# A causal stage's masks move into the copies of turned weights, one product moves to VectorE, and the order is planned from other durations

## The reference

```python
dot = einsum('bhid,bhjd->bhij', q, k)                       # 16 heads of 16
vals = q_norm_sq + k_norm_sq.transpose(0, 1, 3, 2)
scores = dot * dot / (vals - 2.0 * dot + EPSILON)
scores = scores + triu(ones, k=1) * -1000000000.0           # causal
attn = softmax(scores, axis=-1)
out = einsum('bhij,bhjd->bhid', attn, v)
```

## Time and profile before

| | us |
|---|---|
| median of 3 runs | 5082.77 (5076.04 to 5086.52) |
| the profiled execution | 5068.32 |
| its span, first to last instruction | 5066.3 |
| PE, DVE, ACT, POOL busy | 4401.1, 3392.7, 2583.0, 2323.3 |
| TensorE clock, mean over the span | 0.924 of full |

### The profile page before, as it was taken

How to read it: one execution, slowest core, us unless ns; L and a number is a source line. 1 busy time by engine, 2 the same in 40 slices (tenths; PEclk the granted TensorE clock), 3 DMA queues, 4 the chain that set the end, 5 groups by cost and what they waited for, 6 DMA issues and landing times.

```text
span 5066.3 us, 65767 instructions
## 1 busy us (share of the span) xinstructions
PE 4401.1 (87%) x23008; PEld 2677.9 (53%) x23008; DVE 3392.7 (67%) x7648; ACT 2583.0 (51%) x5513; POOL 2323.3 (46%) x2203
## 2 busy tenths in 40 slices
PE   7888888999999999987787777777799999999997
PEld 3444445555555555554554454444555555555564
DVE  4454466666666666647889988999766666656553
ACT  4344344444444444427887777777444444444442
POOL 1111145455454454534555555565545444455441
PEclk9999999999999999997777777887899999999998
DMA  2000000000001000000000000100000000000000
GB/s 65 9 5 5 9 22 11 3 3 5 20 3 31 7 9 11 16 16 17 20 20 17 16 22 18 32 11 15 29 3 3 5 20 9 25 15 17 11 15 21
DMA packets 61208, 77.56 MB, mean 15 GB/s; under 512 B 13896, under 2 KB 45264, under 8 KB 60880
## 3 DMA queue, kind: packets, MB, share of 16 engines
q1 hardware_dynamic: 60880, 73.36, 5.0%
HBM read 35.61 MB, written 12.58 MB: 10 GB/s over the span
## 4 chain that ended last, share of the span: by engine, by line
PE 61%; DVE 21%; issue 7%; ACT 6%; POOL 4%; DMA 1%; SPq 1%; DVEq 0%; POOLq 0%; ACTq 0%
PE wide L725 44%; PE o_ps L725 8%; PE turn_ps L728 5%; PE wide L728 3%; DVE prob L1262 3%; DVE x L1256 2%; DVE pt L1299 2%; DVE prob L1273 2%; DVE hid L1256 1%; DVE x L1143 1%; DMA shifted<-resid 1%; DVE st L1280 1%; ACT pt L1106 1%; POOL rn L1443 1%; DVE w_up L1239 1%
## 5 line engine op out<-in xcount | busy, mean ns | idle before, releaser
L1477 POOL TENSOR_SCALAR prob<-prob,st 128x256 f32<-128x256 f32 (+1 forms) x1024 | 524.8, 533 | 976.9 <-DVE st L1286 976.6
L725 PE MATMUL wide<-x,w_up 128*128 128x512 f32 (+5 forms) x2560 | 943.5, 593 | 21.6 <-DVE k_t L1203 11.4
L725 PE MATMUL wide<-w_in,x_t 128*128 128x512 f32 (+1 forms) x1792 | 828.9, 607 | 6.5 <-DVE w_up L1246 3.1
L725 PE MATMUL o_ps<-pt,v 128*64 128x256 f32 (+2 forms) x5632 | 619.7, 369 | 118.6 <-DVE pt L1299 77.0
L1106 ACT ACTIVATE pt<-turn_ps 128x512 f32<-128x512 f32 x384 | 229.2, 597 | 854.1 <-PE turn_ps L728 854.1
L725 PEld LDWEIGHTS o_ps<-pt,v 128*64 128x64 f32 (+1 forms) x5632 | 394.6, 140 | 380.1 <-issue 191.2
L1075 ACT ACTIVATE prob<-prob,st 128x256 f32<-128x256 f32 (+1 forms) x1024 | 479.0, 472 | 194.7 <-DVE st L1273 194.5
L728 PE MATMUL turn_ps<-ident,prob 128*128 128x128 f32 x2816 | 465.3, 285 | 125.6 <-ACT pt L1106 121.9
L725 PEld LDWEIGHTS wide<-x,w_up 128*128 128x128 f32 (+2 forms) x2560 | 365.1, 200 | 375.5 <-issue 354.4
L728 PEld LDWEIGHTS turn_ps<-ident,prob 128*128 128x128 f32 x2816 | 315.1, 142 | 420.1 <-issue 238.0
L725 PEld LDWEIGHTS wide<-w_in,x_t 128*128 128x128 f32 x1792 | 339.9, 200 | 370.4 <-issue 363.8
(11 more groups left out here) (132 smaller groups left out, 7823.2 us busy)
## 6 DMA issues: line engine op xcount, KB each, us to landing
kept<-resid SPq DMA_DIRECT2D x16, 512.0 KB, 2.6
x<-kept SPq DMA_DIRECT2D x16, 512.0 KB, 3.3
...
```

Source lines behind the costliest of these rows:

```text
L725: return eng.matmul(out, lhsT, rhs, start=start, stop=stop, skip_group_check=True)
L1477: last = eng.tensor_scalar(pr[:, local_span(t)], pr[:, local_span(t)], sm[:, 8 + t:9 + t], 1.0, ALU.mult, ALU.mult)
```

## The change

It does four things. (1) `bclose` moves from POOL's queue to DVE's, one `tensor_tensor` over 768, 768 or 1024 columns. (2) `mask` is gone. The blocks on the diagonal are instead transposed into the half that DVE copies, and DVE's `pt_b` multiplies them by `causal_keep` (the transposed mask) as it reads them from PSUM; where that half holds other blocks too (i % 3 = 2), a second instruction copies these. (3) `B_TURNS` shares the blocks of both heads anew between the copies: ACT's takes 2, 4, 4 blocks for the three sorts of step (before 3, 3, 4), DVE's 4, 2, 4, of which 4, 2, 2 are masked. `turned_to` tells `mix` where a block lies. (4) All durations in `cost` are replaced, for stages a and f too, and the order of all queues is planned anew.

```diff
+B_TURNS = [([(0, 0), (1, 0)], [(0, 1), (0, 2), (1, 1), (1, 2)]),
+           ([(0, 0), (0, 1), (1, 0), (1, 1)], [(0, 2), (1, 2)]),
+           ([(0, 0), (0, 1), (1, 0), (1, 1)], [(0, 3), (1, 3), (0, 2), (1, 2)])]
+B_OWN = [4, 2, 2]
+def turned_to(i, k, block):
+    for half in range(2):
+        if (k, block) in B_TURNS[i % 3][half]:
+            return 512 * half + P * B_TURNS[i % 3][half].index((k, block))
...
-        return 2.8 if i % 2 else 0.0
+        return {"score": {"a": 1.92, "f": 1.72}, "mix": {"a": 2.4, "f": 1.68}}[kind][st] if i % 2 else 0.0
...
-            put("mask", k, at + 1 / steps, final("exp", k))
             for side in "ab":
-                put("turn_" + side, k, at + 2 / steps, final("mask", k))
+                put("turn_" + side, k, at + 2 / steps, final("exp", k))
...
                 elif kind in ("turn_a", "turn_b") and stage_of(u) == "b":
-                    pe.wait_ge(S["mask"], nth("mask", u, i))
-                    at, to = (0, 0) if kind == "turn_a" else (b_width(i), 512)
-                    for kb in range(b_width(i) // P):
-                        last = tr(ps[:, to + kb * P:to + (kb + 1) * P],
-                                  prob[SLOTS[u, i]["prob"]][:, at + kb * P:at + (kb + 1) * P])
+                    pe.wait_ge(S["exp"], nth("exp", u, i))
+                    for k, block in B_TURNS[i % 3][kind == "turn_b"]:
+                        to, at = turned_to(i, k, block), k * b_width(i) + block * P
+                        last = tr(ps[:, to:to + P], prob[SLOTS[u, i]["prob"]][:, at:at + P])
...
+                elif kind == "bclose":
+                    den, inv = [a[(o - 1) % 3][:, 0:2 * b_width(i)] for a in (b_den, b_inv)]
+                    dve.wait_ge(S["bguess"], o)
+                    eng.tensor_tensor(den, den, inv, ALU.mult).then_inc(S["bclose"], 1)
...
-                    w = {"f": 384, "a": 512, "b": b_width(i)}[stage_of(u)]
-                    ps = wide[PLACE["turn_b", u, i]][:, 512:1024] if stage_of(u) == "b" else turn_ps
-                    eng.tensor_copy(pt[:, 512:512 + w], ps[:, 0:w]).then_inc(S["pt_b"], 1)
+                    if stage_of(u) == "b":
+                        ps, met, n = wide[PLACE["turn_b", u, i]], P * B_OWN[i % 3], P * len(B_TURNS[i % 3][1])
+                        last = eng.tensor_tensor(blocks(pt[:, 512:512 + met]), blocks(ps[:, 512:512 + met]),
+                                                 causal_keep[:, :].unsqueeze(1).to_broadcast([P, met // P, P]), ALU.mult)
+                        if n > met:
+                            last = eng.tensor_copy(pt[:, 512 + met:512 + n], ps[:, 512 + met:512 + n])
+                        last.then_inc(S["pt_b"], 1)
...
-                elif kind == "bclose":
-                    pool.wait_ge(S["bguess"], o)
-                    eng.tensor_tensor(den, den, inv, ALU.mult).then_inc(S["bclose"], 1)
-                elif kind == "mask":
-                    pool.wait_ge(S["exp"], nth("exp", u, i))
-                    eng.tensor_tensor(at, at, ones, ALU.mult).then_inc(S["mask"], 1)
```

More of the change, by code:

```diff
@@ L89 @@
         "ACT": "xt_c raw v_c q_c aq_c lat_c av_c bsq bk_c bq_c bnum bguess exp pt_a out olog gelu",
-        "DVE": "bn_h nrm_h cos ss join k_c ak_c row bss bclip bmul low inv pt_b out_b res bn_f bn_f2 nrm_f xt2_c gate hid res2",
-        "POOL": "rstd_h sin rn brow bias_b bclose mask wt rstd_f bias back rot pad_out pad_down pad_v",
+        "DVE": "bn_h nrm_h cos ss join k_c ak_c row bss bclip bclose bmul low inv pt_b out_b res bn_f bn_f2 nrm_f xt2_c gate hid res2",
+        "POOL": "rstd_h sin rn brow bias_b wt rstd_f bias back rot pad_out pad_down pad_v",
         "SP": "load_in load_out load_rot load_up kept moved back_in store dup_a dup_b"}.items():
@@ L94 @@
         ENGINE[_k] = _e
-B_COST = {"bclip": (0.15, 0.27), "bnum": (0.1, 0.22), "bguess": (0.2, 0.47), "bclose": (0.2, 0.6), "bmul": (0.8, 0.6),
-          "exp": (0.85, 0.21), "turn_a": (0.03, 0.175), "turn_b": (0.03, 0.175), "pt_a": (0.06, 0.12),
-          "pt_b": (0.12, 0.135), "mix": (0.05, 0.34), "mask": (0.95, 0.0)}
+B_COST = {"bclip": (0.3, 0.27), "bnum": (0.1, 0.23), "bguess": (0.2, 0.48), "bclose": (0.1, 0.27), "bmul": (0.5, 0.53),
+          "exp": (0.85, 0.24), "mix": (0.05, 0.33)}
 def cost(kind, u, i):
@@ L105, in cost @@
     if kind in ("score", "mix") and st != "b":
-        return 2.8 if i % 2 else 0.0
+        return {"score": {"a": 1.92, "f": 1.72}, "mix": {"a": 2.4, "f": 1.68}}[kind][st] if i % 2 else 0.0
+    if kind in ("turn_a", "turn_b", "pt_a", "pt_b") and st == "b":
+        n = len(B_TURNS[i % 3][kind[-1] == "b"])
+        return {"turn": 0.03 + 0.17 * n, "pt_a": 0.1 + 0.12 * n, "pt_b": (0.26 if i % 3 == 2 else 0.13) + 0.135 * n}[
+            "turn" if kind[0] == "t" else kind]
     if kind in B_COST and st == "b":
@@ L109, in cost @@
     if kind in ("bden", "bdot"):
[L110 removed]
+        return 0.05 + 0.34 * b_width(i) / P if kind == "bdot" else 0.0
     by_stage = {
[L112 to L114 removed]
[3 rows of a table added]
     if kind in by_stage:
         return by_stage[kind][st]
[L117 to L125 removed]
+    flat = {"xt": 0.95, "qk": 3.7, "vv": 3.7, "spread": 0.93, "aq": 3.7, "lat": 1.85, "ak": 1.9, "av": 1.9, "bqkv": 3.7,
+            "bk": 0.65, "bq": 0.65, "proj": 1.72, "xt2": 1.06, "up_g": 3.55, "up_h": 3.55, "down": 2.6, "sel": 0.65,
+            "xt_c": 1.2, "raw": 2.04, "v_c": 1.03, "q_c": 0.6, "aq_c": 1.03, "lat_c": 0.6, "av_c": 1.03, "bsq": 0.93,
+            "bk_c": 0.57, "bq_c": 0.57, "out": 0.6, "olog": 1.2, "out_b": 2.4,
+            "gelu": 5.6, "bn_h": 2.3, "nrm_h": 1.5, "cos": 2.08, "ss": 1.62, "join": 2.63, "k_c": 0.68, "ak_c": 1.23,
+            "row": 0.95, "bss": 0.8, "res": 1.23,
+            "bn_f": 1.11, "bn_f2": 1.79, "nrm_f": 2.9, "xt2_c": 1.6, "gate": 1.49, "hid": 1.49, "res2": 1.23,
+            "rstd_h": 1.02, "sin": 3.14, "rn": 3.05, "brow": 1.8, "bias_b": 2.4,
+            "rstd_f": 1.01, "bias": 2.38, "back": 2.5, "rot": 4.0, "pad_out": 1.0, "pad_down": 0.3, "pad_v": 4.0}
     return flat.get(kind, 0.2)
@@ L487 @@
         "aq aq_c lat lat_c ak ak_c av av_c bqkv row bsq bv bss brow bk bk_c bq bq_c bias_b "
-        "score bden bdot low inv exp wt wt_b bclip bnum bln bguess bclose binv bmul turn_a turn_b mask neg pt_a pt_b mix sel out olog oexp osum out_b "
+        "score bden bdot low inv exp wt wt_b bclip bnum bln bguess bclose binv bmul turn_a turn_b neg pt_a pt_b mix sel out olog oexp osum out_b "
         "proj res moved bn_f bn_f2 var_f rstd_f nrm_f bias xt2 xt2_c up_g gate gelu up_h hid down res2 back_in back store "
@@ L1296, in vector_program @@
                     pt = prob_t[SLOTS[u, i]["pt"]]
[L1297 to L1299 removed]
+                    if stage_of(u) == "b":
[5 more added lines that the diff above has]
+                        last.then_inc(S["pt_b"], 1)
+                    else:
+                        w = {"f": 384, "a": 512}[stage_of(u)]
+                        eng.tensor_copy(pt[:, 512:512 + w], turn_ps[:, 0:w]).then_inc(S["pt_b"], 1)
                 elif kind == "out_b":
@@ L1652, in constants @@
         "local_mask": np.concatenate([previous, own], axis=1),
-        "causal_floor": np.where(j > i, DEN_MAX, DEN_MIN), "causal_ones": np.where(j > i, 0.0, 1.0),
+        "causal_floor": np.where(j > i, DEN_MAX, DEN_MIN), "causal_keep": np.where(i > j, 0.0, 1.0),
         "sum_rows": np.where(i == j - j % BROW + BHD, 1.0, 0.0),
```

30 lines of the change are left out of this document (4 added, 26 removed), and 3 rows, old and new, of the table by_stage.

## The result

The changed kernel takes 4919.6 us, the median of 4 runs (4918.1 to 4935.4), against 5079.4 (5070.0 to 5086.5) for the kernel before: ratio 0.970, 95% interval 0.968 to 0.972. The profiled execution of after took 4935.4 us with a span of 4933.2; the pair of profiled spans differs by 133 us.

What follows compares the result with a forecast made beforehand. TensorE was taken to bound stages f, and VectorE, held up by GpSimd on a shared port, stage b. Stage b's -101 and stages f's +30 gave -71 us: 4997 profiled, 5012 as median, range 4935 to 5078.

Steps and rivals of the forecast that it cites:

- the sum of VectorE's busy time in stage b: Stage b: VectorE's busy time becomes 1144 - 240 + 188 + 8 = 1100 us.
- the +30 for stages f: Stages f: new TensorE waits less those taken away sum to +35 us over 27 units, taken as +30.
- 240 of 246 us go: Stage b: of VectorE's 246 us spent behind GpSimd, about 240 go when `bclose` and `mask` leave GpSimd.
- the moved product (+198 gross, +188 net): Stage b: `bclose` on VectorE costs 198 us for 192 instructions, less some 10 us for overlap of neighbours.
- copies (+8): Stage b: VectorE's masked copies `pt_b` cost 8 us more, between 0 and +15; ScalarE's `pt_a` nothing.
- idle time (60): Stage b: VectorE's idle time falls from 117 to 60 us, by 24 for GpSimd waits and 33 for TensorE waits.
- rival (C): Stage b: slower, as `bclose` on VectorE's queue waits for ScalarE's first reciprocal; total +77 to +151 us, chance 0.13.
- rival (A): Stage b gains more: VectorE busy 1086 us, idle 20, stage 1106, total 4958 us; chance 0.18.
- The three new waits: Stages f, TensorE, each unit: second `vv` 1.8 us, second `up_h` 1.3, `turn_b` right behind its `turn_a` 0.69.
- Rival (B): Stages f do not lose: added waits are covered by ones that go; total 4972 us, chance 0.18.
- Stage a and passages (0, within 10): Stage a keeps its order and changes by nothing; passages between stages change by 0, within 10 us either way.
- I added 14.5 us: Whole kernel: the profiled execution before lay 14.5 us below its median, so 4997 us profiled becomes 5012.

Runs made afterwards that it cites:

- Experiment 5: The changed kernel with extra GpSimd products on constants in each step of stage b, which nobody waits for: 5124.5 us, ratio 1.010 to the kernel before.
- (1): The changed kernel with the planner's former durations for stages a and f put back, so only stage b is new: 4922.3 us, ratio 0.970 to the kernel before.
- (2): The kernel before with only the new planner durations for stages a and f: 5102.3 us, ratio 1.005 to the kernel before.
- (3): The changed kernel with the mask still on GpSimd behind the exp, so only `bclose` moves to VectorE: 4977.9 us, ratio 0.981 to the kernel before.
- (4): The changed kernel with `bclose` still on GpSimd, so only the masks move into the copies: 4980.7 us, ratio 0.982 to the kernel before.
- (6): The changed kernel once more, unaltered: 4921.8 us, ratio 0.969 to the kernel before.
- (9): The changed kernel with `spread` 3 put back behind the second `down` in each f unit: 4918.2 us, ratio 0.969 to the kernel before.
- (7): The changed kernel with the planner's tie for parts of stage f widened from 0.05 to 0.3 us: 5055.1 us, ratio 0.996 to the kernel before.

## Why the prediction was wrong, step by step

The prediction gave 5012 us and the kernel takes 4920. The mechanism that it named for stage b held: VectorE was held up by GpSimd's instructions, and was so no more. The step that failed most is the sum of VectorE's busy time in stage b, forecast at 1100 us and measured at 1065: the excess was summed over two kinds of instruction, where others held 30 us more of it, and the overlap of neighbours, put at 10 us, grew by 29. The second is the +30 for stages f, measured at +4: the waits came, but the sum put TensorE's clock at nothing. 30 us more are how far the two profiled executions lay from their medians, which is chance.

- **Stage b, VectorE's excess (step: 240 of 246 us go).** It held, within 7 us, for the two groups that I summed: the product with the row maximum went from 421.4 us of group busy time to 231.7, the corrected reciprocal from 244.3 to 201.0, together -233. Experiment 5 brings the excess back without any hand-over. What failed is that the sum stopped at these two groups. Others of VectorE's instructions that read and write SBUF paid as well: the output's two (L1305 and L1308: 28.4 + 25.5 us, now 43.0), the normed rows (L1143: 794 and 803 ns, now 403 to 405), the rotary products of projections (L1194, L1197: 2161 and 1768 ns, now 1217 and 1224), and a few small ones. Together these groups are 37 us shorter. Some 7 us of that are only fewer instructions in the stretch (L1194 and L1197 have 4 where 5 were, L1180 has 9 where 12 were, the row sum L1187 has 4 where 6 were); some 30 us are excess that was in the trace and not in my sum. Not all paid: a row sum (L1226, 407 and 409 ns) and the norm statistics (L1153, 407 and 411 ns), both with one input in SBUF, kept their times. The Trainium skill (SBUF — State Buffer, section "SBUF: two separate sides") names as bound to the port every VectorE instruction with two inputs in SBUF or in a two-port mode; read so, it would have sent me through all the groups. The trace agrees for the forms with two inputs in SBUF, which all got shorter, and the groups with an input in PSUM didn't move (683 and 685, 410 and 412, 944 and 949 ns). That L1143, with one input, runs in such a mode is shown by no row here.
  The dearest of these groups, VectorE's of before in stage b (as in the earlier trace rows, which doesn't have them):

```profile
L1305 DVE SCALAR_TENSOR_TENSOR shifted<-o_t,shifted 128x512 f32<-128x512 f32 x31 | 28.4, 915 | 1.1
L1308 DVE SCALAR_TENSOR_TENSOR o_t<-w_down,shifted 128x512 f32<-128x512 f32 x31 | 25.5, 822 | 1.1
...
L1143 DVE TENSOR_SCALAR turned<-resid,stat_h 128x256 f32<-128x256 f32 x16 | 11.8, 794 | 0.0
L1194 DVE TENSOR_TENSOR turned<-turned,sines 128x1024 f32<-128x1024 f32 x5 | 10.8, 2161 | 0.0
...
L1197 DVE TENSOR_TENSOR turned<-turned,rn 128x1024 f32<-128x1024 f32 x5 | 8.8, 1768 | 0.2
...
L1143 DVE TENSOR_SCALAR resid<-resid,stat_h 128x256 f32<-128x256 f32 x8 | 6.0, 803 | 0.0
```

- **Stage b, the moved product (+198 gross, +188 net).** 206 gross. The shortest instruction of the earlier trace rows was the right price for 768 columns (957 against 940); the 1024-column one averages 1312 against 1206. The overlap with neighbours was undersized: over all of VectorE, group busy times add up to 98.7 us more than its busy time before and to 127.3 after, 28.6 more where I took 10.
- **Stage b, copies (+8).** 112.1 us became 96.9 + 26.4 = 123.3: +11.
- **Sum of VectorE's busy time (1100).** 1065: -79 where -44 was forecast. The terms: -233 + 206 + 11 - 37 - 29, and +3 in the rest. This is the step that failed most.
- **Stage b, idle time (60).** 47. No wait for the first reciprocal: 3.4 us in all, so rival (C) fell; its cover, thin by my count (5.1 against 5.7 us a step), was enough. The clip's waits for TensorE fell from 48.5 to 11.2 us; I had taken 33 off. Busy and idle together make 1112: in the stage's time that is close to rival (A)'s 1106, which had a busy time of 1086 and an idle time of 20. That is luck: the gain came from busy time that (A) didn't have, and the idle time didn't fall to its 20.
- **Stages f (+30).** The three new waits came as written: the square 23.3 us in 13 units (1.8 each), `hid` 15.3 in 13 (1.2 each), `turn_b` behind `turn_a`, and the wait of `xt2` for the normed rows went from 15.3 to 4.7. TensorE's idle time rose by 12.7 and by 16.8 us, which is the +30. But the stages grew by 4 and 0, because its busy time fell by 8.6 and 16.8 for the same matmuls. Rival (B), that f doesn't lose, came true by a way that it didn't name, and so by luck.

The way is TensorE's clock. Before, in an f unit at its last step's `turn_b`: first TensorE's timeline (start us, us), then three stretches with the granted clock, as a share of 2.4 GHz, in the third column from the right:

```profile
1135.88 0.55 PE L728 MATMUL turn_ps<-ident,prob 128*128 128x128 f32 x3 [2.08 <-ACT pt L1106]
1136.27 5.30 PE L725 MATMUL wide<-w_in,x_t 128*128 128x512 f32 x8
```

```profile
1134.00:1137.00 3.00, 1.11 (x5) 0.77 (x6) 2.54 (x3) 3.00 (x9) 2.76 (x3) 1.00 0.01 3
1137.00:1140.40 3.40, 3.40 (x5) 1.33 (x4) 1.68 (x4) 0.67 (x4) 3.11 (x2) 0.50 0.00 0
1140.40:1144.00 3.60, 3.60 (x21) 1.73 (x20) 1.34 (x2) 2.40 (x3) 3.60 (x6) 1.00 0.00 0
```

After, at the same place of a unit:

```profile
1152.48 0.55 PE L745 MATMUL turn_ps<-ident,prob 128*128 128x128 f32 x3 [2.08 <-ACT pt L1122]
1152.87 3.60 PE L742 MATMUL wide<-w_in,x_t 128*128 128x512 f32 x8
```

```profile
1149.50:1152.40 2.90, 0.90 (x6) 0.37 (x4) 1.34 (x2) 2.40 (x4) 2.66 (x5) 1.00 0.01 3
1152.40:1155.80 3.40, 3.31 (x10) 1.72 (x11) 3.37 (x6) 1.87 (x9) 3.12 (x3) 1.00 0.00 0
```

The wait is the same, 2.08 us, and the eight matmuls behind it are the same; they take 5.30 us in one and 3.60 in the other, since behind the wait the clock is at 1.2 GHz for 3.4 us before and stays at 2.4 GHz after. By TensorE's timeline, 17 of 27 such waits of `turn_b` in the f stages of the kernel before are followed by half speed, and 2 of 25 in the changed kernel. By the record of the granted clock that is 27 and 41 us at half speed over the two f stages, and 14 and 7 in the changed kernel. At 1.7 us of TensorE's time for each 3.4 us at half speed, as in these rows, the 14 and 34 us less are worth 7 and 17 us, against the 8.6 and 16.8 that the busy time fell by. It goes with the order, and not with the single execution: with the former order of f it is 27 + 38 in (1), with the new one 14 + 3 in (2), 14 + 10 in (3), 14 + 7 in (4), 14 + 0 in (5) and 17 + 10 in (6). Which part of the order does it is open. The place of `spread` 3 alone isn't it (9), and neither are the instructions next to the wait: in the kernel before another unit has the same ones at 1229 us, with the same wait of 2.08 us, and its eight matmuls take 3.60 us.

- **Stage a and passages (0, within 10).** Stage a took 779 us against 769 in the profiled run, at 96 us of half clock against 78 (and began 1 us later); in the runs of the experiments it went with the half clock too, from about 760 us with 55 at half clock (3) to 774 with 85 (7). The passages: -4, +4 and +1. Together +12.
- **The profiled execution against the median.** I added 14.5 us because before's lay that far below its median. After's lay 15.8 above it, so that 30 us of the miss are this alone, and no mechanism of the change. The whole miss, 5012 - 4920 = 92 us, is 48 (stage b) + 26 (f) - 12 (a and passages) + 30.

The time lies 15 us below the range. The least busy time that the prediction allowed was 1086 us, the bound of the groups summed, with nothing for a group left out, and that is 21 us above the 1065 measured. With 21 us more of busy time, or without the 30 us between profiled executions and medians, the time would have fallen within the range.
